# Exponentials of the attention stage: one step at a time, or two steps in one instruction behind two tanh

## The chip, the core and the metric

The kernel runs on one core of a Trainium2 chip. Its five engines work side by side, each through its own queue in order, and wait for each other by semaphores: TensorE (PE in the profile, PEld its weight loads), VectorE (DVE), ScalarE (ACT), GpSimd (POOL) and SyncE (SP), which here only issues transfers. The metric is the device time of one execution in microseconds (us), median of several runs.

## The reference, cut to what matters

Two layers of a small model, each an attention-like half times a gate. The first layer's attention is the part at hand: 4 sequences of 512 tokens, 8 heads, two sets of queries and keys of 8 dimensions per head.

```python
L1 = jnp.einsum('bhnd,bhmd->bhnm', _l2norm(q1), _l2norm(k1)) * cos_scale
L2 = jnp.einsum('bhnd,bhmd->bhnm', _l2norm(q2), _l2norm(k2)) * cos_scale
G = jnp.tanh(delta_gain.reshape(1, H, 1, 1) * (L1 - L2))
A1 = jax.nn.softmax(L1 + G, axis=-1)
A2 = jax.nn.softmax(L2 - G, axis=-1)
attn = A1 - lambda_full * A2
y = jnp.einsum('bhnm,bhmd->bhnd', attn, v)
```

The first layer's gate holds a mixture of 8 experts, one expert per token (`relu(x @ W1[e] + b1[e]) @ W2[e] + b2[e]`). Its blocks of 128 tokens run in between the steps of the attention. The second layer, a state-space model of four sublayers and another mixture of experts, comes behind it and isn't touched.

## The kernel before, in words

The attention stage runs over four pairs of heads (`pair_of_heads`: q = -1 unrolled and named `first`, q = 0 and 1 as a loop, q = 2 named `final`). A pair has 32 **steps**, a step being 128 keys by 512 queries of one head and one sequence. Four steps make a **unit** (one head and one sequence), so there are 32 units. From the second pair on, each unit u also carries one expert block: 24 units with a block, 8 without.

The work of step n:
- TensorE `difference` (L817): the differences L1 - L2 into `bank_d`, of which there are two; it waits until the tanh of step n - 2 has read the bank. `scores` (L822, L823): both logits into `bank_l`, two as well, free when VectorE has summed step n - 2.
- ScalarE `gate` (L923): tanh of `bank_d` into `gt`, a ring of 4. `exps` (L929 before): exponentials of `tt`, 1024 columns, into `ex`.
- VectorE `sums` (L978, L979): L1 + G and L2 - G (from the negated second logits) into `tt`, a ring of 4.

The work of unit u, done while later steps run:
- TensorE `weigh` (L863), in two halves of two steps: the values weighted by `ex`, into the single bank `bank_pv`.
- ScalarE `keep` (L934 before): a copy of `bank_pv` into `pvs`, behind the second half of weigh.
- TensorE `turn` (L871): four transposes of `pvs` back into `bank_pv`. VectorE `settle` (L986) reads them, and only then may the next unit's weigh begin.

The work of the expert block of unit u:
- TensorE `turn_block` (L838) into `bank_e`; ScalarE `keep_in` (L938 before) copies it to `block_inT`; TensorE `hidden` (L844); VectorE `relu` (L994); TensorE `block_out` (L850); ScalarE `keep_out` (L943 before) copies the result, and frees `bank_e` for the next block.

The order on each engine is written out by hand in the loops over steps. On TensorE, step st issues `difference` of st + 2, then `scores` of st + 1; at the first step of unit u also turn(u - 2) and turn_block(u), at the second hidden(u) and the first half of weigh(u - 1), at the third block_out(u) and the second half of weigh(u - 1). Here `pair_of_heads` runs u within a pair; a unit's turn is of the unit whose copy was made last.

Of the kernel before, what the change touches and what calls it, by code (L numbers as in the profile page):

```python
# [8 lines left out]
ACT = mybir.ActivationFunctionType  # L9
# [38 lines left out]
def build_stages(nc, A, out):  # L48
    keep = ExitStack()
    with keep:  # L50
        def sb(stack, name, shape, dtype=fp32):
            return stack.enter_context(nc.sbuf_tensor(name, shape, dtype))
# [22 lines left out]
        with keep0:  # L75
# [39 lines left out]
            with st1:  # L115
# [51 lines left out]
                with nc.Block() as block:  # L167
# [15 lines left out]
                    @block.sync  # L183
                    def _(sp):
                        for b in range(B):
                            sp.dma_start(X[:, 4 * b:4 * b + 4, :], A["x"][b].rearrange("(k p) d -> p k d", p=P)).then_inc(s_x[b], 16)
                        for dst, src in first_loads:
                            sp.dma_start(dst, src).then_inc(s_w, 16)
                        for dst, src in small_loads:
                            sp.dma_start(dst, src).then_inc(s_w2, 16)  # L190
                        for dst, src in loads:
                            sp.dma_start(dst, src).then_inc(s_w3, 16)
                        for h in range(NH):
                            sp.dma_start(sub_col[16 * h:16 * h + 16, :], A["subln"].rearrange("(d o) -> d o", o=1)).then_inc(s_b2l, 16)
                        sp.wait_ge(s_b2z, 1)
                        for t in range(NT):
                            sp.dma_start(b2blk[NE * t:NE * t + NE, t, :], A["b2"]).then_inc(s_b2l, 16)

                        for b in range(B):
                            sp.wait_ge(s_mid, 2 * b + 2)  # L200
                            sp.wait_ge(s_loq, b + 1)
                            sp.wait_ge(s_lok, b + 1)
                            for n, w in enumerate("qk"):
                                for i in range(3):
                                    sp.dma_start(columns(qk_dram[n, i], b), columns(parts[w, i], b)).then_inc(s_qkst, 16)
                        sp.wait_ge(s_qkst, 16 * 6 * B)
                        sp.wait_ge(s_z, 2)
                        for part in range(2):
                            load_part(sp, 0, 0, part, s_hl)
                        sp.wait_ge(s_hl, 16 * LOADS)  # L210
                        sp.wait_ge(s_b2l, 16 * (NT + NH))
# [420 lines left out]
            with st2:  # L632
                RING = 4
# [28 lines left out]
                tt = sb(st2, "tt", [P, RING, 2, 512])  # L662
                ex = sb(st2, "ex", [P, 2, 4, 2, 512])
# [9 lines left out]
                s_D, s_L, s_G, s_T, s_E = map(sem, ("diff_in_psum", "logits_in_psum2", "gate_ready", "sums_ready", "exp_ready"))  # L673
# [8 lines left out]
                LEAD, STEPS, UNITS, PER = 4, 32, 8, BLOCKS // 3  # L682
                step = lambda q, n: LEAD + STEPS + STEPS * q + n
# [5 lines left out]
                with nc.Block() as block:  # L689
# [220 lines left out]
                    @block.scalar  # L910
                    def _(act):
                        for s in (s_G, s_E, s_pvs, s_xk, s_ek):
                            act.sem_inc(s, LEAD)
                        for s in s_es:
                            act.sem_inc(s, 16)

                        def gate(q, st):
                            i = (st // 16) % 2
                            if st % 16 == 0:
                                act.wait_ge(s_dg, q * 2 + (st // 16 + 3))  # L920
                            act.wait_ge(s_D, step(q, st + 1))
                            act.wait_ge(s_T, step(q, st - RING + 1))
                            nc.scalar.activation(gt[:, st % RING, :], bank_d[st % 2][:, :], ACT.Tanh, scale=dgh[:, i:i + 1]).then_inc(s_G, 1)  # L923

                        def exps(q, st):
                            act.wait_ge(s_T, step(q, st + 1))
                            if st % 4 == 0:
                                act.wait_ge(s_pvd, unit(q, st // 4 - 1))
                            nc.scalar.activation(ex[:, (st // 4) % 2, st % 4, :, :], tt[:, st % RING, :, :], ACT.Exp).then_inc(s_E, 1)  # L929

                        def keep(q, u):
                            act.wait_ge(s_pvd, unit(q, u + 1))
                            act.wait_ge(s_pvt, unit(q, u))
                            nc.scalar.activation(pvs[:, :], bank_pv[:, :], ACT.Copy).then_inc(s_pvs, 1)  # L934

                        def keep_in(q, k):
                            act.wait_ge(s_xt, blk(q, k + 1))
                            nc.scalar.activation(xbT[:, :], bank_e[:, 0, :], ACT.Copy).then_inc(s_xk, 1)  # L938

                        def keep_out(q, k):  # L940
                            act.wait_ge(s_dn, blk(q, k + 1))
                            act.wait_ge(s_es[k % 2], loaded(q, k))
                            nc.scalar.activation(eo[k % 2][:, :], bank_e[:, 0, :], ACT.Copy).then_inc(s_ek, 1)  # L943

                        def pair_of_heads(q, first=False, final=False):
                            for st in range(STEPS):
                                u, mb = st // 4, st % 4
                                if not (final and st == STEPS - 1):
                                    gate(q, st + 1)
                                if not (first and st == 0):  # L950
                                    exps(q, st - 1)
                                if mb == 3 and not (first and u == 0):
                                    keep(q, u - 1)
                                if mb == 0 and not first:
                                    keep_in(q, u)
                                if mb == 3 and not first:
                                    keep_out(q, u)

                        gate(-1, 0)
                        pair_of_heads(-1, first=True)  # L960
                        with act.Fori(0, 2) as q:
                            pair_of_heads(q)
                        pair_of_heads(2, final=True)
                        exps(2, STEPS - 1)
                        keep(2, UNITS - 1)

                    @block.vector
# [971 lines left out]
        with st5:  # L1939
# [34 lines left out]
            first = lambda l, b: isinstance(l, int) and l == 0 and b == 0  # L1974
# [601 lines left out]
```

## Time and profile before

| | |
|---|---|
| device time, median of 3 runs | 1323.59 us (1323.31 to 1324.79) |
| span of the profiled execution (no device time is listed for it alone) | 1331.0 us |
| mean granted TensorE clock | 0.945 of 2.4 GHz |
| TensorE busy in the span | 1161.9 us (87%) |
| VectorE busy | 1103.2 us (83%) |
| ScalarE busy | 1051.4 us (79%) |
| GpSimd busy | 914.3 us (69%) |
| exps, 128 of 128x1024 | 138.4 us busy, 1081 ns mean |
| tanh, 128 of 128x512 | 91.3 us busy, 714 ns mean |

The span runs from the first to the last instruction that the profiler saw. The busy shares are means over stages with different limits: the attention stage lies between about 104 and 356 us of it and has limits of its own. A busy time of TensorE counts its pipelined matmuls with modelled ends, so that the distance between starts says more than the durations. The granted clock has two levels here, 1.00 (2.4 GHz) and 0.50 (1.2 GHz).

### The profile page before, as it was taken

Reading aid. Unit: us, or ns where it says so; the run is one execution under the profiler, and the core shown is the slowest. Engines: PE = TensorE matmul, PEld = TensorE weight load, DVE = VectorE, ACT = ScalarE, POOL = GpSimd, SP = SyncE. Lnnn points to the kernel's source line nnn. Section 1 sums busy time; section 2 is a strip of 40 time slices with the busy share of each in tenths; the row PEclk is TensorE's granted clock in tenths of the full one; section 3 lists DMA queues with packets and bytes.
Section 4 is the critical chain, followed back from the end, with each engine's and each line's share of the span. In section 5 each row is a group of like instructions: output and inputs, shape, how many; then the busy total and the mean of one; then the engine's idle time right before and its main releaser. Section 6 shows DMA issues by size and latency. Waiting matters only on the chain. (4 is left out here: it accounts for less than half of the span.)

```text
span 1331.0 us, 21677 instructions
## 1 busy us (share of the span) xinstructions
PE 1161.9 (87%) x6667; PEld 613.7 (46%) x6667; DVE 1103.2 (83%) x1535; ACT 1051.4 (79%) x1868; POOL 914.3 (69%) x749
## 2 busy tenths in 40 slices
PE   6566799999818999987999999999999999999885
PEld 4461144444414565663444444444444444444442
DVE  7966698999785323338999999999999999999997
ACT  4347799999743224359899999999999999999992
POOL 6734212111284442347999999999999999999995
PEclk9776799999966999998999999999999999999998
DMA  2122223433107305523345234423441444144420
GB/s 70 33 86 96 74 86 104 123 111 114 34 22 253 130 17 130 150 68 103 76 104 124 66 68 108 105 77 77 104 109 55 93 106 109 49 88 103 105 65 16
DMA packets 89061, 120.20 MB, mean 90 GB/s; under 512 B 17869, under 2 KB 49464, under 8 KB 88576
## 3 DMA queue, kind: packets, MB, share of 16 engines
q1 hardware_dynamic: 82688, 101.59, 30.0%
q0 software_dynamic: 6272, 17.38, 4.5%
q8 instruction: 48, 0.79, 0.3%
q14 instruction: 53, 0.43, 0.1%
HBM read 92.28 MB, written 27.45 MB: 90 GB/s over the span
## 5 line engine op out<-in xcount | busy, mean ns | idle before, releaser
L2094 POOL TENSOR_TENSOR hcm<-hs,Cc 128x1024 f32<-128x1024 f32 x255 | 600.8, 2379 | 27.5 <-DVE hs L2477 23.1
L2477 DVE TENSOR_TENSOR_SCAN hs<-decay,dbx 128x512 f32<-128x512 f32 x512 | 586.8, 1200 | 25.5 <-ACT decay L2370 9.5
L2211 PEld LDWEIGHTS dbx<-ident_sb,scaled 128*128 128x128 f32 x2048 | 227.7, 142 | 288.4 <-DVE hs L2477 164.4
L2211 PE MATMUL dbx<-ident_sb,scaled 128*128 128x128 f32 x2048 | 312.3, 283 | 41.4 <-DVE hs L2477 38.1
L2352 ACT ACTIVATE scaled<-duT,BT 128x256 f32<-128x256 f32 x579 | 266.9, 506 | 0.2 <-PE dbx L2211 0.2
L2370 ACT ACTIVATE decay<-dtr_even,a_all 128x512 f32<-128x512 f32 x256 | 178.6, 721 | 3.0 <-DVE hs L2477 1.7
L2370 ACT ACTIVATE decay<-dtr_odd,a_all 128x512 f32<-128x512 f32 x256 | 177.9, 721 | 2.3 <-DMA dtr_odd<-dt_turn 1.5
L929 ACT ACTIVATE ex<-tt 128x1024 f32<-128x1024 f32 x128 | 138.4, 1081 | 5.5 <-DVE tt L979 5.1
L2229 PE MATMUL y_bank<-hcm,fold_sb 128*32 128x512 f32 x1024 | 139.5, 617 | 2.1 <-POOL hcm L2094 2.1
L2142 PE MATMUL slots<-XT,w_tap 128*128 128x512 f32 (+1 forms) x224 | 115.4, 597 | 3.1 <-DVE scaled L2468 2.7
L978 DVE TENSOR_TENSOR tt<-bank_l,gt 128x512 f32<-128x512 f32 x128 | 87.4, 683 | 27.9 <-PE bank_l L823 19.2
L923 ACT ACTIVATE gt<-bank_d,dgh 128x512 f32<-128x512 f32 x128 | 91.3, 714 | 17.1 <-issue 7.6
L2079 POOL TENSOR_SCALAR scaled<-duT,BT 128x256 f32<-128x256 f32 x204 | 96.2, 485 | 0.0
L979 DVE SCALAR_TENSOR_TENSOR tt<-bank_l,gt 128x512 f32<-128x512 f32 x128 | 87.0, 680 | 0.0
L863 PE MATMUL bank_pv<-ex,v_head 128*32 128x512 f32 x512 | 72.1, 638 | 3.3 <-issue 2.8
L1839 DVE TENSOR_TENSOR hid<-sil,u_bank 128x512 f32<-128x512 f32 x32 | 22.0, 688 | 58.5 <-ACT sil L1696 30.8
L2468 DVE TENSOR_TENSOR scaled<-slots,BT 128x1024 f32<-128x1024 f32 (+1 forms) x60 | 67.8, 1131 | 0.0
L752 POOL CAST weight_rows<-w_row 128x1 uint32 (+1 forms) x24 | 4.5, 187 | 82.7 <-PE bank_e L850 82.7
L746 POOL COPY dgh<-delta_gain_sb 128x1 f32<-128x1 f32 (+1 forms) x8 | 1.4, 184 | 80.0 <-PE bank_pv L863 59.8
L1696 ACT ACTIVATE sil<-g_bank 128x512 f32<-128x512 f32 x32 | 19.1, 597 | 46.9 <-PE u_bank L1553 41.3
L1929 DVE TENSOR_TENSOR hid<-sil,u_bank 128x320 f32<-128x320 f32 x32 | 15.6, 488 | 48.7 <-ACT sil L1782 40.0
L1517 POOL DMA_INDIRECT shares_of_tokens<-eo,to_u x18 | 17.2, 956 | 51.8 <-ACT eo L1819 48.2
(379 smaller groups left out, 1938.0 us busy)
## 6 DMA issues: line engine op xcount, KB each, us to landing
Cc<-bc_turn SPq DMA_DIRECT2D x256, 64.0 KB
dtr_even<-dt_turn SPq DMA_DIRECT2D x32, 512.0 KB, 8.6
dtr_odd<-dt_turn SPq DMA_DIRECT2D x32, 512.0 KB, 8.4
dt_turn<-dt SPq DMA_DIRECT2D x16, 512.0 KB, 2.8
hid<-in_conv_row SPq DMA_DIRECT2D x4, 512.0 KB, 5.9
shares_of_tokens<-zeros SPq DMA_DIRECT2D x2, 1024.0 KB, 8.1
w_rg<-in_w_rg SPq DMA_DIRECT2D x8, 256.0 KB
w_ru<-in_w_ru SPq DMA_DIRECT2D x8, 256.0 KB
```

The source lines that it names most:

```text
L923: nc.scalar.activation(gt[:, st % RING, :], bank_d[st % 2][:, :], ACT.Tanh, scale=dgh[:, i:i + 1]).then_inc(s_G, 1)
L929: nc.scalar.activation(ex[:, (st // 4) % 2, st % 4, :, :], tt[:, st % RING, :, :], ACT.Exp).then_inc(s_E, 1)
L978: nc.vector.tensor_tensor(tt[:, st % RING, 0, :], bank_l[st % 2][:, 0, :], gt[:, st % RING, :], ALU.add)
L979: nc.vector.scalar_tensor_tensor(tt[:, st % RING, 1, :], bank_l[st % 2][:, 1, :], -1.0, gt[:, st % RING, :], ALU.mult, ALU.subtract).then_ ...
L2079: nc.gpsimd.tensor_scalar(scaled[buffer_of(l, n, k)][:, kk, :, j, :], duT[:, n % 2, kk, :].rearrange("p (g c) -> p g c", c=32), BT[:, n % ...
L2094: nc.gpsimd.tensor_tensor(hcm[:, r - 1:r + 1, :], hs[:, p % HR - 1:p % HR + 1, :], Cc[:, k:k + 1, :].broadcast_to([P, 2, 512]), ALU.mult). ...
L2142: last = mm(dst[h][:, d:512], w_tap[:, 3 - d, P * h:P * h + P], XT[:, n % 4, 0:512 - d], start=(d == 0), stop=(d == 3))
L2211: last = nc.tensor.transpose(dbx[bank_of[p]][:, P * kk:P * kk + P], scaled[buffer_of(l, b, k)][:, kk, g, :, :].rearrange("p j c -> p (j c) ...
L2229: last = mm(y_bank[h][32 * q:32 * q + 32, :], fold[:, :], hcm[:, ring_of(l, b, p + q), :], start=False, stop=(k == 3), tile_position=(0, 3 ...
L2352: nc.scalar.activation(scaled[buffer_of(l, n, k)][:, kk, :, j, :], duT[:, n % 2, kk, :].rearrange("p (g c) -> p g c", c=32), ACT.Copy, sca ...
L2370: nc.scalar.activation(dec[:, p % DR, :], dtr[b % 2][:, g, :], ACT.Exp, scale=a_all[:, l, 4 * g + k:4 * g + k + 1]).then_inc(s_dec, 1)
L2477: nc.vector.tensor_tensor_scan(hs[:, p % HR, :], dec[:, p % DR, :], dbx[bank_of[p]][:, :], 0.0, ALU.mult, ALU.add).then_inc(s_sc, 1)
```

## The change

ScalarE's code alone is changed. One instruction takes the exponentials of two steps, 2048 columns, and waits for the sums of both. Ahead of it stand the tanh of the next two steps. The copies of a unit move with it: `keep` and `keep_out` stand behind the exponentials of the unit's third and fourth step, `keep_in` stands behind two tanh and ahead of the exponentials.

```diff
-                        def exps(q, st):
-                            act.wait_ge(s_T, step(q, st + 1))
+                        def exps_of_two(q, st):
+                            act.wait_ge(s_T, step(q, st + 2))
                             if st % 4 == 0:
                                 act.wait_ge(s_pvd, unit(q, st // 4 - 1))
-                            nc.scalar.activation(ex[:, (st // 4) % 2, st % 4, :, :], tt[:, st % RING, :, :], ACT.Exp).then_inc(s_E, 1)
+                            i, j = st % RING, st % 4
+                            nc.scalar.activation(ex[:, (st // 4) % 2, j:j + 2, :, :], tt[:, i:i + 2, :, :], ACT.Exp).then_inc(s_E, 2)
...
                         def pair_of_heads(q, first=False, final=False):
-                            for st in range(STEPS):
+                            for st in range(0, STEPS, 2):
                                 u, mb = st // 4, st % 4
-                                if not (final and st == STEPS - 1):
-                                    gate(q, st + 1)
-                                if not (first and st == 0):
-                                    exps(q, st - 1)
-                                if mb == 3 and not (first and u == 0):
-                                    keep(q, u - 1)
+                                if not (final and st == STEPS - 2):
+                                    gate(q, st + 2)
+                                    gate(q, st + 3)
                                 if mb == 0 and not first:
                                     keep_in(q, u)
-                                if mb == 3 and not first:
+                                exps_of_two(q, st)
+                                if mb == 2 and not (first and u == 0):
+                                    keep(q, u - 1)
+                                if mb == 2 and not first:
                                     keep_out(q, u)
 
                         gate(-1, 0)
+                        gate(-1, 1)
                         pair_of_heads(-1, first=True)
                         with act.Fori(0, 2) as q:
                             pair_of_heads(q)
                         pair_of_heads(2, final=True)
-                        exps(2, STEPS - 1)
                         keep(2, UNITS - 1)
```

On ScalarE, in the loop over pairs, from the exponentials of a unit's third step to the next unit's first exponentials, before the change (`gt` is written by the tanh, `ex` by the exponentials, `pvs` by `keep`, `block_out` by `keep_out`, `block_inT` by `keep_in`):

```order
L929 ACTIVATE ex<-tt 128x1024
L932 REGISTER_ALU
L934 ACTIVATE pvs<-bank_pv 128x512
L942 ISA
L943 ACTIVATE block_out<-bank_e 128x128
L921 REGISTER_ALU
L923 ACTIVATE gt<-bank_d,dgh 128x512
L929 ACTIVATE ex<-tt 128x1024
L937 REGISTER_ALU
L938 ACTIVATE block_inT<-bank_e 128x128
```

The tanh of the next unit's second step stands behind both copies, and one step's exponentials lie between the copies of `keep` and `keep_in`. The same place after the change, from that same tanh of the next unit's second step on:

```order
L923 ACTIVATE gt<-bank_d,dgh 128x512
L930 ACTIVATE ex<-tt 128x2048
L933 REGISTER_ALU
L935 ACTIVATE pvs<-bank_pv 128x512
L943 ISA
L944 ACTIVATE block_out<-bank_e 128x128
L921 REGISTER_ALU
L923 ACTIVATE gt<-bank_d,dgh 128x512
L921 REGISTER_ALU
L923 ACTIVATE gt<-bank_d,dgh 128x512
L938 REGISTER_ALU
L939 ACTIVATE block_inT<-bank_e 128x128
```

That tanh and the exponentials of two steps now stand ahead of `keep`, and two tanh stand between `keep_out` and `keep_in`. On TensorE the order is the same before and after; from block_out of a unit to hidden of the next it reads:

```order
L850 MATMUL bank_e<-expert_weights,hid 128x128 x4
L863 MATMUL bank_pv<-ex,v_head 32x512 x4
L816 REGISTER_ALU
L817 MATMUL bank_d<-XT 128x512
L822 MATMUL bank_l<-XT 128x512
L823 MATMUL bank_l<-XT 128x512
L816 REGISTER_ALU
L817 MATMUL bank_d<-XT 128x512
L822 MATMUL bank_l<-XT 128x512
L823 MATMUL bank_l<-XT 128x512
L869 REGISTER_ALU
L871 MATMUL bank_pv<-ident_sb,pvs 128x128 x4
```

The first `bank_d` here is the one that the tanh of the next unit's second step reads; nothing moved, and it stands behind block_out and weigh and ahead of the turn.

## Rows read from the trace of the kernel before

**Rows 1.** Windows: us busy by engine (PE, PEld, DVE, ACT, POOL), PEclk, DMA.

```profile
168.00:350.80 182.80, 179.88 (x1194) 84.65 (x1186) 167.50 (x354) 174.67 (x269) 30.22 (x54) 1.00 0.34 102
```

**Rows 2.** Timeline of TensorE, one unit: start us, us, what, [idle before <-releaser].

```profile
200.82 1.06 PE L863 MATMUL bank_pv<-ex,v_head 128*32 128x512 f32 x8
201.82 0.39 PE L817 MATMUL bank_d<-GATE 112*128 112x512 bf16 x1
...
203.10 0.66 PE L871 MATMUL bank_pv<-ident_sb,pvs 128*128 128x128 f32 x4
203.60 0.27 PE L838 MATMUL bank_e<-ident_sb,block_in 128*128 128x128 f32 x1
203.71 0.38 PE L817 MATMUL bank_d<-GATE 112*128 112x512 bf16 x1
...
204.46 1.16 PE L844 MATMUL bank_e<-block_inT,expert_weights 128*128 128x128 f32 x8
205.55 1.06 PE L863 MATMUL bank_pv<-ex,v_head 128*32 128x512 f32 x8
206.55 0.39 PE L817 MATMUL bank_d<-GATE 112*128 112x512 bf16 x1
206.87 0.39 PE L822 MATMUL bank_l<-GATE 48*128 48x512 bf16 x1
...
207.19 1.16 PE L850 MATMUL bank_e<-expert_weights,hid 128*128 128x128 f32 x8
208.28 1.06 PE L863 MATMUL bank_pv<-ex,v_head 128*32 128x512 f32 x8
209.27 0.39 PE L817 MATMUL bank_d<-GATE 112*128 112x512 bf16 x1
```

**Rows 3.** Timeline of ScalarE in the same unit.

```profile
201.95 0.60 ACT L934 ACTIVATE pvs<-bank_pv 128x512 f32<-128x512 f32 x1 [0.34 <-PE bank_pv L863]
...
204.12 0.28 ACT L938 ACTIVATE block_inT<-bank_e 128x128 f32<-128x128 f32 x1
...
204.92 1.05 ACT L929 ACTIVATE ex<-tt 128x1024 f32<-128x1024 f32 x1
205.87 0.68 ACT L923 ACTIVATE gt<-bank_d,dgh 128x512 f32<-128x512 f32 x1
206.44 1.05 ACT L929 ACTIVATE ex<-tt 128x1024 f32<-128x1024 f32 x1
...
209.41 0.60 ACT L934 ACTIVATE pvs<-bank_pv 128x512 f32<-128x512 f32 x1 [0.25 <-PE bank_pv L863]
```

**Rows 4.** Groups by line and form: busy us, mean ns, idle before.

```profile
L2383 ACT ACTIVATE GATE<-GATE 128x2048 f32<-128x2048 f32 x1 | 1.9, 1919 | 0.0
```

**Rows 5.** Timeline of ScalarE, copies of units without expert blocks.

```profile
159.06 0.66 ACT L934 ACTIVATE pvs<-bank_pv 128x512 f32<-128x512 f32 x1
...
165.61 0.70 ACT L934 ACTIVATE pvs<-bank_pv 128x512 f32<-128x512 f32 x1
```

**Rows 6.** Timeline of TensorE around three waits for ScalarE.

```profile
158.35 0.39 PE L817 MATMUL bank_d<-GATE 112*128 112x512 bf16 x1 [0.53 <-ACT gt L923]
...
159.78 0.93 PE L871 MATMUL bank_pv<-ident_sb,pvs 128*128 128x128 f32 x4 [0.72 <-ACT pvs L934]
...
163.47 0.39 PE L817 MATMUL bank_d<-GATE 112*128 112x512 bf16 x1
...
172.94 0.66 PE L871 MATMUL bank_pv<-ident_sb,pvs 128*128 128x128 f32 x4 [0.72 <-ACT pvs L934]
```

**Rows 7.** Timeline of ScalarE, one wait early in the stage.

```profile
144.44 0.69 ACT L923 ACTIVATE gt<-bank_d,dgh 128x512 f32<-128x512 f32 x1 [7.61 <-issue]
```

**Rows 8.** Windows of 1 us: columns as in the first group.

```profile
159.00:160.00 1.00, 0.28 (x4) 0.23 (x3) 1.00 (x2) 1.00 (x3) 0.00 (x0) 1.00 0.05 20
162.00:163.00 1.00, 1.00 (x8) 0.00 (x0) 1.00 (x3) 1.00 (x2) 0.00 (x0) 0.50 0.00 0
173.00:174.00 1.00, 1.00 (x8) 0.66 (x8) 0.20 (x1) 1.00 (x2) 0.00 (x0) 1.00 0.00 0
```

## The prediction

> **What bounds the attention stage now.** I first read the busy shares of the stage from the second pair of heads on, 168 to 350.8 us [rows 1]: TensorE 179.9 of 182.8 us at the full granted clock, ScalarE 174.7, VectorE 167.5. All three are nearly full, so a change of order on one of them has to be followed through the others. Then I read one unit in order of time. A unit is four steps; I write D(n), L(n) for the difference and score matmuls of step n, G(n) for its tanh (`gate`), T(n) for VectorE's sums, and "exps" for the exponentials.
>
> TensorE runs, in a fixed order: at step 4u D(4u+2), L(4u+1), turn(u-2), the block's turn; at 4u+1 D(4u+3), L(4u+2), hidden(u), first half of weigh(u-1); at 4u+2 D(4u+4), L(4u+3), block_out(u), second half of weigh(u-1); at 4u+3 D(4u+5), L(4u+4). In the trace one unit lasts from the second half of weigh at 200.82 to the next at 208.28, 7.46 us, and the starts follow each other almost without a gap [rows 2]. TensorE is the bound, but by little.
>
> ScalarE's row for the same unit shows what the change touches [rows 3]. `keep` copies the values at 201.95, as soon as weigh ends, and is done at 202.55; G(4u+5) comes behind it. The turn that needs the copy starts at 203.10 [rows 2]: it has 0.55 us to spare. That number decides this case.
>
> **The change, part by part.** It removes 128 exps of 1024 columns and adds 64 of 2048. ScalarE starts its next instruction 0.95 us after an exps of 1024 columns that lasts 1.05, so 0.10 is overlapped [rows 3]. No exps of 2048 columns is in the trace; a Silu of 2048 columns, from SBUF to SBUF as the exps are, lasts 1.919 us [rows 4]. The bounds are twice the exps, 2.10, and the exps plus the step from a 512-column to a 1024-column instruction, 1.05 + (1.05 - 0.68) = 1.42. I take 1.92, the row of the same width, since another function on the same columns is nearer than another width. Less 0.10 it occupies 1.82, against 2 x 0.95 = 1.90: 0.08 saved per pair, 64 x 0.08 = 5.1 us if ScalarE alone decided.
>
> It moves two things, and these cost. In the old order G(4u+4), exps(4u+2), keep(u-1), keep_out(u) stood before G(4u+5). In the new order G(4u+4), G(4u+5), exps(4u+2 and 4u+3) stand before keep(u-1). G(4u+5) reads D(4u+5), and D(4u+5) stands on TensorE behind block_out(u) and the second half of weigh(u-1). ScalarE works in order, so it stands still in front of G(4u+5) until TensorE has finished that weigh, although the sums for the exps are long there; then it does G, then 1.82 us of exps, and only then the copy that turn(u-1) waits for. Before, D(4u+5) started at 201.82 and the copy at 201.95 [rows 2, 3]. After, the copy starts a tanh and an exps pair behind the end of D(4u+5). Meanwhile TensorE can only run L(4u+4), D(4u+6), L(4u+5), and then it waits at turn(u-1). Second, keep_in(u+1) now stands behind G(4u+6) and G(4u+7), and D(4u+7) stands on TensorE behind that same turn; so hidden(u+1), which needs keep_in, is late again.
>
> The new cycle, each from a start to the next start, runs from D(4u+5) to D(4u+9):
> D to G: 0.39 for D plus 0.07, the time from the end of weigh (208.28 + 1.06) to the copy at 209.41 [rows 2, 3]: 0.46.
> G to exps 0.57 (205.87 to 206.44) [rows 3]; exps pair to keep 1.82; keep to turn 0.72, from 159.06 to 159.78 in a unit where the turn did wait for it, less the 0.06 by which that copy lasted longer (0.66 against 0.60): 0.66 [rows 3, 5, 6].
> Turn to the block's turn to D(4u+7) 0.61; D to G(4u+7) 0.46; G to keep_in 0.57; keep_in to hidden 0.34 (204.12 to 204.46) [rows 2, 3].
> Hidden to weigh 1.09, weigh to D 1.00, D to L 0.32, L to block_out 0.32, block_out to weigh 1.09, weigh to D(4u+9) 0.99 [rows 2].
> Sum: 0.46 + 0.57 + 1.82 + 0.66 + 0.61 + 0.46 + 0.57 + 0.34 + 1.09 + 1.00 + 0.32 + 0.32 + 1.09 + 0.99 = 10.30 us. Against 7.46 that is 2.84 us a unit, and there are 24 units with expert blocks: 24 x 2.84 = **68.2 us**. The bounds of the exps move it by about 3 us up and, at 1.32 occupied, by 12 us down.
>
> The first eight units have no expert blocks. There the cycle is D to G 0.46, G 0.57, exps 1.82, keep to turn 0.66, turn 0.50, D and L 0.64, weigh 1.00, D and L 0.64, weigh 0.99: 7.28 us. In the old order these units took 6.55 us (copies at 159.06 and 165.61) [rows 5], ScalarE alone being full. So 0.73 for each of units 4 to 7, **2.9 us**. Units 1 to 3 lie ahead of a wait of 7.61 us at 144.44 that the profile explains by nothing it shows [rows 7]; it may absorb their loss. I take 0 for them and 8 as the other end, since VectorE's settle between the sums isn't in my cycle.
>
> **The clock.** The new unit leaves TensorE two gaps: D(4u+5), L, D, L last 4 x 0.32 = 1.28 us while the turn starts 0.46 + 0.57 + 1.82 + 0.66 = 3.51 after D(4u+5), a gap of 2.2 us; and before hidden another, 1.37 from D(4u+7) less 0.64 for D and L, 0.7 us. What gaps do here: after one of 0.72 us before the turn at 159.78, with another of 0.53 shortly ahead of it, the granted clock went from 1.00 to 0.50 (2.4 to 1.2 GHz), and the turn, D, L and weigh took 3.69 us to the D at 163.47 [rows 6, 8]. At full clock the same four take 0.50 + 0.32 + 0.32 + 1.00 = 2.14 [rows 2]. One such fall costs 1.55 us. After the same wait of 0.72 at 172.94 the clock stayed at 1.00 [rows 6, 8]. The new gaps are over twice as long, so falls are likely but not certain in each unit. Bounds: none, 0; one in each of 31 units, 48 us. I take two units in three of the 24: 16 x 1.55 = **25 us**, nearer to the upper end, as the gaps are nearer to those that brought the fall.
>
> **Sum.** 68.2 + 2.9 + 24.8 = 95.9 us. The stage ends later by that, and what follows begins only when the last engine has left the stage, so all of it is passed on. The profiled span of 1331.0 us is 7.4 above the median of the runs, 0.6%; I add the difference to the median: 1323.6 + 95.9 = **1420 us**.
>
> **Rivals.** *The clock stays up.* The same late copy, no falls: 1323.6 + 68.2 + 2.9 = 1395. For it: the unit of 172.94. Against it: the fall at 159.78 after shorter gaps. *The clock falls in every unit, the first ones too:* 68.2 + 8 + 48 = 124, so 1448, and more if a second fall comes in a unit.
>
> *The saving decides, faster.* ScalarE is 174.7 of 182.8 us busy, and if only its throughput counted, 5.1 us would be gained: 1318.5. It would come so if turn(u-1) could bear the later copy. It becomes later by the end of D, G and the exps pair, 201.82 + 0.46 + 0.57 + 1.82 = 204.67 against 201.95, which is 2.72 us, and the turn has 0.55 to spare; the exps pair would have to occupy under 0 us for that. I see no mechanism that gives it, save that ScalarE's wait in front of G(4u+5) isn't the one I read.
> On this the Trainium skill, "Perfetto Trace Analysis", section Optimizing Scalar/DVE Operations, says both: grouping into larger operations helps a saturated engine, and where an engine isn't saturated but causes bubbles on others, breaking up lets work end sooner. By its first half the time would be the 1318.5 of this rival; by its second the change goes the wrong way, and the trace bears out the second, with 0.55 us of slack at the turn.
>
> *No change:* TensorE would have to take in 2.84 us a unit from idle time that it has already; in the whole stretch it idles 182.8 - 179.9 = 2.9 us [rows 1].
>
> **Chances.** Late copy with falls of the clock in part of the units 0.55; with hardly any 0.25; in every unit or worse 0.14; faster 0.04; no change 0.02. The range reaches into both slower rivals: from 1384, the 1395 less most of the 12 us of the exps' lower bound, to 1452, a little over the worst case's 1448. A measurement of this kernel tells about 0.2% from no change: faster 0.04, same 0.02, slower 0.94.
>
> **What would show it.** In the changed trace: exps of 2048 columns of about 1.92 us; ScalarE idle about 2 us before every fourth tanh, released by bank_d; TensorE idle about 2.2 us before the turn, released by the copy, and 0.7 before hidden, released by block_inT; units of 10.3 us at full clock; the granted clock below 1 in parts of 168 to 440 us. Wrong would be: units under 9 us, a copy that starts before the exps pair's end, or falls of the clock that last through the stage.

## The result

The changed kernel takes 1458.85 us (median of 4 runs, 1454.41 to 1462.38) against 1324.19 us before (4 runs): 1.101 times as long, 95% interval 1.0986 to 1.1035. It is slower, as forecast, but by 134.7 us in place of 95.9, and outside the range, which ended at 1452.

The page of the changed kernel gives the busy time of each engine, and the groups by line and form of the attention stage give the two instructions of ScalarE (columns: busy us, mean ns of one, idle before and what ended it):

```profile
span 1458.6 us, 21645 instructions
...
PE 1220.8 (84%) x6667; PEld 639.8 (44%) x6667; DVE 1105.4 (76%) x1535; ACT 1052.3 (72%) x1804; POOL 915.2 (63%) x749
```

```profile
L930 ACT ACTIVATE ex<-tt 128x2048 f32<-128x2048 f32 x64 | 122.0, 1906 | 23.7 <-DVE tt L980 12.4 <-issue 11.3
...
L923 ACT ACTIVATE gt<-bank_d,dgh 128x512 f32<-128x512 f32 x128 | 87.7, 688 | 127.8 <-PE bank_d L817 117.2 <-DVE tt L980 10.7
```

An exps pair (the exponentials of two steps in one instruction) takes 1.906 us; the forecast took 1.92 from [rows 4]. What is new is the idle time ahead of the tanh, 127.8 us, of which 117.2 end when TensorE's `bank_d` arrives: ScalarE stands still there.

One unit of the loop, in order of time, answers to [rows 2] and [rows 3]. TensorE from the turn of one unit to the turn of the next (start us, us, what, in brackets the idle time before and what ended it):

```profile
280.05 0.66 PE L871 MATMUL bank_pv<-ident_sb,pvs 128*128 128x128 f32 x4 [2.10 <-ACT pvs L935]
...
282.06 2.07 PE L844 MATMUL bank_e<-block_inT,expert_weights 128*128 128x128 f32 x8 [0.70 <-ACT block_inT L939]
284.06 1.94 PE L863 MATMUL bank_pv<-ex,v_head 128*32 128x512 f32 x8
...
287.01 1.64 PE L850 MATMUL bank_e<-expert_weights,hid 128*128 128x128 f32 x8
288.58 1.06 PE L863 MATMUL bank_pv<-ex,v_head 128*32 128x512 f32 x8
289.58 0.39 PE L817 MATMUL bank_d<-XT 112*128 112x512 bf16 x1
...
293.03 0.65 PE L871 MATMUL bank_pv<-ident_sb,pvs 128*128 128x128 f32 x4 [2.10 <-ACT pvs L935]
```

ScalarE in the same unit:

```profile
290.01 0.69 ACT L923 ACTIVATE gt<-bank_d,dgh 128x512 f32<-128x512 f32 x1 [2.67 <-PE bank_d L817]
290.59 1.90 ACT L930 ACTIVATE ex<-tt 128x2048 f32<-128x2048 f32 x1
292.39 0.59 ACT L935 ACTIVATE pvs<-bank_pv 128x512 f32<-128x512 f32 x1
```

The forecast chain is there link by link. ScalarE waits 2.67 us for the D(4u+5) that TensorE starts at 289.58, behind block_out and weigh. G starts at 290.01 (0.43 after D), the pair 0.58 later, the copy 1.80 later, the turn 0.64 later. TensorE waits 2.10 us at the turn and 0.70 at hidden; the forecast said 2.2 and 0.7.

What the forecast sized wrongly is seen in the durations: hidden 2.07 us where [rows 2] has 1.16, weigh 1.94 where it has 1.06. The windows of the changed kernel (us busy of PE, PEld, DVE, ACT, POOL, then the granted clock, DMA) show why; the last is the whole loop, from the 8th to the 31st copy:

```profile
281.20:287.80 6.60, 5.90 (x24) 2.98 (x23) 4.25 (x10) 3.41 (x4) 0.00 (x0) 0.50 0.20 57
288.00:294.60 6.60, 4.24 (x28) 1.69 (x26) 2.55 (x5) 4.26 (x6) 1.73 (x4) 1.00 0.21 59
294.90:298.00 3.10, 3.04 (x16) 1.99 (x16) 1.75 (x6) 1.92 (x2) 0.00 (x0) 0.50 0.35 115
298.30:304.90 6.60, 4.50 (x30) 1.82 (x27) 4.65 (x9) 3.84 (x6) 1.20 (x2) 1.00 0.29 96
191.46:477.44 285.98, 226.21 (x1120) 106.18 (x1120) 160.46 (x333) 163.72 (x206) 28.31 (x50) 0.77 0.21 64
```

The clock falls to 1.2 GHz in the unit from 281, for over 6.6 us, and again in the next, for half as long. Over the loop its mean is 0.77, where [rows 1] has 1.00. The copies of `keep` on ScalarE give the length of the units; these are the first, the 8th, four in a row from the loop, and the 31st:

```profile
125.80 0.58 ACT L935 ACTIVATE pvs<-bank_pv 128x512 f32<-128x512 f32 x1
...
191.46 0.59 ACT L935 ACTIVATE pvs<-bank_pv 128x512 f32<-128x512 f32 x1
...
404.99 0.59 ACT L935 ACTIVATE pvs<-bank_pv 128x512 f32<-128x512 f32 x1
416.76 0.59 ACT L935 ACTIVATE pvs<-bank_pv 128x512 f32<-128x512 f32 x1
429.60 0.59 ACT L935 ACTIVATE pvs<-bank_pv 128x512 f32<-128x512 f32 x1
442.54 0.59 ACT L935 ACTIVATE pvs<-bank_pv 128x512 f32<-128x512 f32 x1
...
477.44 0.58 ACT L935 ACTIVATE pvs<-bank_pv 128x512 f32<-128x512 f32 x1
```

### The profile page after: what moved, and what is told of

Same layout as the page of the kernel before. It is cut to its first block and busy times, and to the rows that moved or that the text cites. A ratio compares the mean times of both kernels' runs of the same rounds, so it can differ in the third digit from the quotient of the medians.

```text
span 1458.6 us, 21645 instructions
## 1 busy us (share of the span) xinstructions
PE 1220.8 (84%) x6667; PEld 639.8 (44%) x6667; DVE 1105.4 (76%) x1535; ACT 1052.3 (72%) x1804; POOL 915.2 (63%) x749
## 5 line engine op out<-in xcount | busy, mean ns | idle before, releaser
L923 ACT ACTIVATE gt<-bank_d,dgh 128x512 f32<-128x512 f32 x128 | 87.7, 688 | 127.8 <-PE bank_d L817 117.2
L930 ACT ACTIVATE ex<-tt 128x2048 f32<-128x2048 f32 x64 | 122.0, 1906 | 23.7 <-DVE tt L980 12.4
L863 PE MATMUL bank_pv<-ex,v_head 128*32 128x512 f32 x512 | 93.4, 814 | 0.5 <-DVE ybig L987 0.5
L871 PE MATMUL bank_pv<-ident_sb,pvs 128*128 128x128 f32 x128 | 23.7, 313 | 64.7 <-ACT pvs L935 64.7
L987 DVE TENSOR_REDUCE ybig<-bank_pv 128x136 f32<-128x272 f32 (+1 forms) x32 | 14.1, 442 | 71.1 <-PE bank_pv L871 71.1
L844 PE MATMUL bank_e<-block_inT,expert_weights 128*128 128x128 f32 x192 | 49.8, 441 | 13.1 <-ACT block_inT L939 13.1
```

Source lines behind the costliest of these rows:

```text
L863: last = nc.tensor.matmul(bank_pv[32 * j:32 * j + 32, :], vh[i][:, 4 * b + mb, :], ex[:, u % 2, mb, s, :], start=(pair == 0), stop=(pair = ...
L930: nc.scalar.activation(ex[:, (st // 4) % 2, j:j + 2, :, :], tt[:, i:i + 2, :, :], ACT.Exp).then_inc(s_E, 2)
```

## The experiments

Ten other kernels were run, and the kernel before once more. Full clock in what follows is the granted clock 1.00. A unit is the distance of two copies of `keep` on ScalarE; "the loop" is the 23 units from the 8th to the 31st copy.

**The exponentials split again, order kept.**

```diff
-nc.scalar.activation(ex[:, (st // 4) % 2, j:j + 2, :, :], tt[:, i:i + 2, :, :], ACT.Exp).then_inc(s_E, 2)
+for k in range(2):
+    nc.scalar.activation(ex[:, (st // 4) % 2, j + k, :, :], tt[:, i + k, :, :], ACT.Exp).then_inc(s_E, 1)
```

> The changed order on ScalarE is kept, but the exponentials of two steps are again two instructions of 1024 columns, one behind the other. Theory A (the place of the copies behind the second tanh and both exponentials is the cause): the cycle is 10.3 us at full clock as before, 2 x 0.95 in place of 1.82, so the time stays near that of the change, 1450 to 1468 us. Theory B (the merged instruction is the cause, since it waits for the sums of both steps and holds ScalarE for 1.9 us): the time goes most of the way back, under 1350 us.

Measured: 1458.19 us, ratio to before 1.1019 (1.0981 to 1.1057), the same as the change. The merged instruction as such has no part in the loss of this order. Two things are the same in both runs, the order and the wait for the sums of both steps; of the second the changed trace shows little, 12.4 us of idle time ahead of all 64 pairs that VectorE's sums ended. The runs below change the order.

**TensorE's gaps filled with repeated matmuls.** The score matmuls of a step are repeated into the same bank, with the same result, so that TensorE is busy in the gaps. Each run has one of the three added lines; the loop that repeats the matmuls inside `scores` is left out here.

```diff
-scores(q, st + 1)
+scores(q, st + 1, {0: 7, 1: 3}.get(mb, 1))     # both gaps
+scores(q, st + 1, {0: 7, 1: 1}.get(mb, 1))     # the long gap alone
+scores(q, st + 1, {0: 1, 1: 3}.get(mb, 1))     # the short gap alone
```

> The change, with TensorE's two gaps in each unit filled by repeats of work that is done anyway: the score matmuls ahead of the turn run 7 times in place of once (6 x 0.32 = 1.9 us of the 2.1 us gap), those ahead of hidden 3 times (0.64 of 0.7 us). The result is the same numbers. Theory A (of the 4.99 us a unit, 2.8 are the late copy and 2.2 are the granted clock that falls in the gaps): the clock stays at 1.00 in the loop, units last 10.2 to 10.4 us, and the time is 1324 + 24 x 2.85 + 8 = 1400 us (1390 to 1412). Theory B (the extra 2.2 us are something else, such as waits between VectorE and ScalarE that the longer unit brings): units stay at 12 us or more and the time stays at 1450 us or above.

> The change with only the long gap ahead of the turn filled, by six repeats of the score matmuls (1.9 of 2.1 us); the short gap of 0.7 us ahead of hidden stays. If the long gap is what brings the falls, none are left: units of 10.2 us and 1400 to 1406 us, as with both gaps filled. If the short gap brings falls too, units above 11 us and 1415 us or more.

> Only the gap of 0.7 us ahead of hidden is filled, by two repeats of the score matmuls there; the gap of 2.1 us ahead of the turn stays. If the long gap makes the clock fall and the short one behind it keeps it low for twice as long (two of three units are 12.84 us, one is 11.77), every unit comes to 11.8 us or less and the time is 1435 us or less. If the long gap alone decides both, the time stays within 5 us of 1459.

Measured: 1401.01 us with both gaps filled (ratio 1.0582, 1.0564 to 1.06), 1401.07 with the long gap alone (1.0589, 1.0571 to 1.0606), 1412.78 with the short gap alone (1.0656, 1.0625 to 1.0687). More work on TensorE makes the kernel faster by 58 us. Copies of the run with both gaps filled, and windows of a stretch in it:

```profile
234.72 0.59 ACT L937 ACTIVATE pvs<-bank_pv 128x512 f32<-128x512 f32 x1
...
244.92 0.59 ACT L937 ACTIVATE pvs<-bank_pv 128x512 f32<-128x512 f32 x1
...
255.12 0.59 ACT L937 ACTIVATE pvs<-bank_pv 128x512 f32<-128x512 f32 x1
```

```profile
200.00:300.00 100.00, 89.99 (x639) 40.40 (x641) 66.67 (x139) 69.97 (x89) 13.34 (x24) 1.00 0.27 82
```

Units are 10.20 us and the clock is 1.00. The forecast cycle at full clock was 10.30. The repeats fill less than expected, since a repeated pair takes 0.22 us and not 0.32: 0.80 us of the long gap are left. The first, the 8th and the 31st copy of this run, and its turn in between:

```profile
126.30 0.59 ACT L937 ACTIVATE pvs<-bank_pv 128x512 f32<-128x512 f32 x1
...
183.74 0.59 ACT L937 ACTIVATE pvs<-bank_pv 128x512 f32<-128x512 f32 x1
...
255.76 0.66 PE L873 MATMUL bank_pv<-ident_sb,pvs 128*128 128x128 f32 x4 [0.80 <-ACT pvs L937]
...
417.34 0.58 ACT L937 ACTIVATE pvs<-bank_pv 128x512 f32<-128x512 f32 x1
```

The run with the long gap alone filled has the same units and the same clock, in the first line below. The same stretch of the run with the short gap alone filled has TensorE 79.33 us busy at a clock of 0.97, five stretches at half clock in its 23 units and most units at 10.20, in the second line:

```profile
200.00:300.00 100.00, 85.70 (x600) 38.98 (x592) 66.72 (x141) 70.85 (x89) 13.18 (x23) 1.00 0.28 83
200.00:300.00 100.00, 79.33 (x517) 36.65 (x515) 67.06 (x141) 67.47 (x85) 12.40 (x24) 0.97 0.25 76
```

So with this order the short gap alone brings no fall and the long one alone brings few; it takes both for one in every unit. The expectations of the first two runs came true. That of the third, 1435 us or less if the short gap prolongs the stretches, holds in its number, but it reckoned with a fall left in each unit: filling either gap is nearly enough.

**The difference matmul issued earlier.**

```diff
-if not (final and st >= STEPS - 2):
+if mb % 2 == 0 and not (final and st >= STEPS - 2):
     difference(q, st + 2)
 if not (final and st >= STEPS - 1):
     scores(q, st + 1)
+if mb % 2 == 0 and not (final and st >= STEPS - 2):
+    difference(q, st + 3)
```

> ScalarE as in the change; on TensorE the difference matmul that the second tanh waits for is issued two steps' matmuls earlier, behind the scores of the same step and ahead of the expert block and the weighting. Theory A (ScalarE stands still ahead of the second tanh because that matmul lies behind block_out and weigh, and the exponentials are held back with it): the pair of exponentials runs while TensorE does block_out and weigh, the copy follows weigh at once, units come to about 8.8 us at full clock, and the time is 1324 + 24 x 1.4 + 6 = 1363 us, up to 1400 if the clock still falls. Theory B (the copy is late because two steps' exponentials lie ahead of it, whatever the tanh waits for): little changes, 1440 us or more.

Measured: 1373.48 us, ratio 1.0386 (1.0364 to 1.0408). ScalarE's order is that of the change, and 85 of the 135 us are gone. Its timeline in this run, and TensorE's turn behind the copy:

```profile
256.83 1.25 ACT L925 ACTIVATE gt<-bank_d,dgh 128x512 f32<-128x512 f32 x2
258.93 1.91 ACT L932 ACTIVATE ex<-tt 128x2048 f32<-128x2048 f32 x1 [0.85 <-DVE tt L982]
260.75 0.58 ACT L937 ACTIVATE pvs<-bank_pv 128x512 f32<-128x512 f32 x1
```

```profile
261.38 0.66 PE L871 MATMUL bank_pv<-ident_sb,pvs 128*128 128x128 f32 x4 [1.09 <-ACT pvs L937]
```

The two tanh run back to back, and the exponentials wait 0.85 us for the sums in place of 2.67 for the matmul. Units are 8.75 to 8.9 us where the clock holds, 9.16 in the mean. Against the 10.20 us of the change at full clock this gives back about 1.4 us a unit, half of what the change cost there; the rest of the 85 us is the clock, which falls seven times in the loop in place of 23. The expected unit of 8.8 us came out, but not the reason, that the copy follows weigh at once: TensorE's second half of weigh starts at 257.93 here, and the pair only at 258.93. What stays is that the copy comes behind the pair, and TensorE waits 1.09 us for it at the turn, in the last line.

**The copies moved back ahead.** On ScalarE alone: `keep` and `keep_out` between the two tanh; `keep_in` ahead of both; and both moves together.

This is the run with both, its conditions left out. The run with `keep` early leaves `keep_in` where it was, the run with `keep_in` early leaves `keep` and `keep_out`.

```diff
+keep_in(q, u)
 gate(q, st + 2)
+keep(q, u - 1)
+keep_out(q, u)
 gate(q, st + 3)
-keep_in(q, u)
 exps_of_two(q, st)
-keep(q, u - 1)
-keep_out(q, u)
```

> The change with keep and keep_out moved between the two tanh: they stand behind the first tanh of the pair and ahead of the second tanh and the exponentials. keep_in stays behind two tanh. Theory A (two waits make the late unit, the turn's for keep and hidden's for keep_in): the first is gone, the second stays, since keep_in still stands behind the tanh that reads the matmul behind the turn; units come to about 9.4 us at full clock, 1324 + 24 x 1.95 + 2 = 1373 us, up to 1420 with falls of the clock. Theory B (keep alone makes the unit late): units near 7.5 us and a time under 1335 us.

> The change with keep_in alone moved ahead of both tanh; keep and keep_out stay behind the pair of exponentials. The wait ahead of hidden goes and the wait of 2.1 us ahead of the turn stays: about 9.5 us a unit at full clock, 1324 + 24 x 2.05 + 8 = 1381 us if the clock stays up, up to 1420 if the long gap alone brings falls. If one late copy were enough for all of the loss, it would stay at 1450 us.

> As the run with keep early, and keep_in moved ahead of both tanh as well, where the block's turn releases it. Theory A: both waits are gone, what remains is that the exponentials of two steps wait for the later step's sums; units of about 8.25 us at full clock, 1324 + 24 x 0.8 = 1343 us, up to 1375 with falls. Theory B (the merged exponentials cost nothing once the copies are early): units at 7.46 us or less and a time of 1318 to 1326 us.

Measured: 1393.18 us with `keep` early (ratio 1.052, 1.0489 to 1.0551), 1418.89 with `keep_in` early (1.0721, 1.0687 to 1.0756), 1344.50 with both (1.0144, 1.0116 to 1.0172). With one copy late, one gap of about 2.1 us remains, once ahead of hidden and once ahead of the turn; TensorE's waits in the first and in the second:

```profile
253.18 1.16 PE L844 MATMUL bank_e<-block_inT,expert_weights 128*128 128x128 f32 x8 [2.06 <-ACT block_inT L939]
...
262.65 2.08 PE L844 MATMUL bank_e<-block_inT,expert_weights 128*128 128x128 f32 x8 [2.06 <-ACT block_inT L939]
```

```profile
252.73 0.66 PE L871 MATMUL bank_pv<-ident_sb,pvs 128*128 128x128 f32 x4 [2.10 <-ACT pvs L935]
```

The units with `keep` early are 9.46 and 11.02 us in turn: the unit of 262.65 runs hidden at half clock. With `keep_in` early they are 9.50 at full clock and 11.0 to 12.5 with a fall. Windows of the two runs, `keep` early first:

```profile
200.00:320.00 120.00, 96.22 (x577) 46.46 (x577) 80.46 (x170) 80.43 (x105) 15.05 (x30) 0.91 0.27 83
200.00:320.00 120.00, 96.93 (x551) 47.62 (x555) 76.79 (x162) 80.59 (x101) 15.20 (x28) 0.87 0.25 78
```

So either late copy alone costs 2.0 us a unit at full clock, and both together 2.7. With both copies early the clock stays up (1.00 from 200 to 320 us) and a unit is 8.31 us, expected 8.25. TensorE still waits 0.90 us in each, for `keep_in`, which stands behind the pair. The reason given in the expectation, that the pair waits for the later step's sums, isn't in the trace: from 200 to 320 us ScalarE has no idle time ahead of its 30 pairs, and stands still only ahead of `keep`. The number came out, the reason didn't:

```profile
250.09 1.16 PE L844 MATMUL bank_e<-block_inT,expert_weights 128*128 128x128 f32 x8 [0.90 <-ACT block_inT L939]
...
258.40 1.16 PE L844 MATMUL bank_e<-block_inT,expert_weights 128*128 128x128 f32 x8 [0.90 <-ACT block_inT L939]
```

**The difference matmul and the copies both earlier.** TensorE as in the run with the difference matmul earlier; ScalarE `keep_in`, two tanh, `keep`, `keep_out`, the pair (conditions left out).

```diff
+keep_in(q, u)
 gate(q, st + 2)
 gate(q, st + 3)
-keep_in(q, u)
-exps_of_two(q, st)
 keep(q, u - 1)
 keep_out(q, u)
+exps_of_two(q, st)
```

> TensorE issues the difference matmuls two steps at a time (the second ahead of the expert block and the weighting), and ScalarE has keep_in first, then two tanh, keep, keep_out, and the pair of exponentials last. Theory A: units of about 8.0 us at full clock, 1324 + 24 x 0.55 = 1337 us (1328 to 1352), still slower than before, since TensorE was full in the loop and the pair of exponentials can only add waits there. Theory B (the saving on ScalarE shows once nothing waits for the copies): 1312 to 1320 us.

Measured: 1332.66 us, ratio 1.0067 (1.0045 to 1.0088). Two copies, and TensorE's wait between them:

```profile
256.59 0.60 ACT L937 ACTIVATE pvs<-bank_pv 128x512 f32<-128x512 f32 x1 [1.02 <-PE bank_pv L863]
...
259.38 1.16 PE L844 MATMUL bank_e<-block_inT,expert_weights 128*128 128x128 f32 x8 [0.69 <-ACT block_inT L941]
...
264.45 0.60 ACT L937 ACTIVATE pvs<-bank_pv 128x512 f32<-128x512 f32 x1 [1.02 <-PE bank_pv L863]
```

The unit is 7.86 us against 7.46 [rows 2]. It is the best order with pairs in the loop that was tried, and it is still slower than before: TensorE was full there and has nothing to gain, and it waits 0.69 us at hidden in each unit.

**Pairs in the first eight units alone,** the loop as before (`exps_of_two` is added as in the change).

```diff
-pair_of_heads(-1, first=True)
+gate(-1, 1)
+for st in range(0, STEPS, 2):
+    u, mb = st // 4, st % 4
+    gate(-1, st + 2)
+    if mb == 2 and u > 0:
+        keep(-1, u - 1)
+    if st < STEPS - 2:
+        gate(-1, st + 3)
+        exps_of_two(-1, st)
+    else:
+        exps(-1, st)
```

> The kernel before in all but the first pair of heads, the eight units without expert blocks, where ScalarE was full: there the exponentials of two steps are one instruction, with keep ahead of the second tanh. Theory A (the saving of a merged instruction shows only where ScalarE is the bound): units 4 to 7 go from 6.55 to about 6.4 us, 1 us in all, 1323 us; and if the wait of 7.6 us early in the stage, which the changed kernel's trace doesn't have, hangs on where ScalarE's code stands, up to 8 us more, 1315 us. Theory B (merging makes waits for the later step's sums here too): 1325 to 1335 us.

Measured: 1325.23 us, ratio 1.0005 (0.999 to 1.0021), no change that can be told. Its copies:

```profile
126.45 0.59 ACT L941 ACTIVATE pvs<-bank_pv 128x512 f32<-128x512 f32 x1
...
132.81 0.63 ACT L941 ACTIVATE pvs<-bank_pv 128x512 f32<-128x512 f32 x1
...
139.17 0.67 ACT L941 ACTIVATE pvs<-bank_pv 128x512 f32<-128x512 f32 x1
```

These are units of 6.36 us against 6.55 [rows 5]: 0.19 us saved where ScalarE is the bound, 0.10 a pair where the forecast had 0.08. It is there, over some five units, and too small for the measurement. The further 8 us hoped for didn't come.

**The kernel before, profiled once more.**

> The kernel before, unchanged, for a second profile. Theory A (the wait of 7.6 us at ScalarE early in the stage, and the longer wait around it, belong to that one profiled execution: its span of 1331.0 us is 7.4 above the median of the runs): no such wait here, the first eight copies lie about 51 us apart from first to last in place of 59.7, and the span is about 1322 us. Theory B (it is in every execution): the wait is there again and the span is about 1331 us.

Measured: span 1323.2 us, one time of 1324.95. The wait of 7.61 us [rows 7] isn't in this execution. Its first and eighth copy are 53.09 us apart; the third line is the 31st:

```profile
118.76 0.58 ACT L934 ACTIVATE pvs<-bank_pv 128x512 f32<-128x512 f32 x1
...
171.85 0.60 ACT L934 ACTIVATE pvs<-bank_pv 128x512 f32<-128x512 f32 x1 [0.51 <-PE bank_pv L863]
...
342.98 0.60 ACT L934 ACTIVATE pvs<-bank_pv 128x512 f32<-128x512 f32 x1
```

In the profile that the forecast was made from the first and the eighth copy are 59.7 apart. That execution carried a wait that none of the other profiled ones has. It doesn't count in full. The copies on its two sides are 17.18 us apart, 10.6 more than their neighbours, but from the first to the eighth copy that execution is only 6.7 us longer: the second profile has a wait of its own later among these units, on TensorE, for a transfer:

```profile
158.39 0.61 PE L817 MATMUL bank_d<-XT 112*128 112x512 bf16 x1 [2.94 <-DMA XT<-qk_parts]
```

## Why the prediction was wrong in size

Against the second profile of before, the 135.4 us between the spans (1458.6 and 1323.2) fall as follows, by the first tanh and the copies of the two traces. The stage starts 4.2 us later (107.58 against 103.38; nothing ahead of it was changed, in the other runs it lies between 103.37 and 104.81, and what this one execution waited for stays open). From there to the first copy it is 18.2 against 15.4 us, 2.8 more. From the first to the eighth copy 65.66 against 53.09, 12.6 more. In the loop 285.98 against 171.13, **114.9 more**. Behind it 0.9 more.

**The bound and the slack: right.** TensorE was full and the turn had 0.55 us to spare; the traces show the new waits of 2.10 and 0.70 us at the two places named.

**The cycle of 10.30 us: right.** With the gaps filled the clock holds and the unit is 10.20. Of the loop's 114.9 us this is 23 x (10.16 - 7.44) = 62.6; the forecast had 68.2 for 24 units. The runs with the copies early show that it is the order, and the run with the earlier difference matmul shows that the stop ahead of the second tanh is about half of it. One side sum is off and changes nothing: the upper bound of the exps, 2.00 occupied in place of 1.82, moves 24 units by 4.3 us, not by 3.

**The clock: the step that failed.** The forecast took 25 us for it, one fall of 1.55 us in two units of three. Measured, the mean unit is 12.43 us against 10.16 with the gaps filled: 2.27 us a unit, 52 us in the loop. The trace has 23 stretches at half clock in those 23 units, 133 of 286 us in all. Units of 11.77 us are 1.57 over the full-clock unit, which is the price of one fall taken from [rows 6]; the others, two of three, are 12.84 to 12.98, 2.6 to 2.8 over it. So the price of a short stretch was right, the count was too low, and that a stretch can last twice as long wasn't in the sum nor in its upper end, which had one fall of that price in every unit. One of the forecast's own signs of being wrong, "falls of the clock that last through the stage", is there in the loop. With 52 us in the loop and about 8 in the first units, where filling the gaps takes 65.66 us between copies down to 57.44, the clock costs some 60 us in place of 25. The row of 172.94 in [rows 6], where it stayed up, was weighed too heavily: there a wait of 0.72 us stood in the place of these 2.10.

**The first eight units: too low.** Forecast 2.9 us, measured 12.6 + 2.8. Of the 12.6, 8.2 go with the clock, as said, and 4.4 stay with the gaps filled (57.44 against 53.09). At full clock the unit there is 7.81 us (the distance most found with the gaps filled) against 6.54, 1.27 a unit where the forecast took 0.73; VectorE's settle, named there as left out, lies in that cycle. The units 1 to 3 lose like the others: the wait of 7.61 us that might have absorbed them belongs to one execution. Seven such units would make 8.9 us and not 4.4; a likely reason is the wait of 2.94 us for a transfer in the kernel before, which the trace with the gaps filled, later by then, doesn't have.

**The rivals.** That the saving decides is out, as the early copies show too: with both copies early and the matmul too the pairs still cost 0.4 us a unit in the loop. None of the kernels tried is faster than the one before. Of the two sentences of the Trainium skill weighed there ("Perfetto Trace Analysis", Optimizing Scalar/DVE Operations), on larger operations and on breaking them up, neither is what decided here: breaking up the pair without moving it left the time at 1458.19 us. "The clock falls in every unit" was held at 0.14 and is what happened, at 1448 by the forecast's price and 1459 measured.

Which gaps bring a fall, and which make a stretch last twice as long, is only partly settled. In the loops with gaps of 0.69, 0.80 and 0.90 us the clock stays at 1.00; with one of about 1.1 it falls seven times in 23 units. It takes both gaps for the pattern of the changed kernel, but one gap of 2.06 ahead of hidden brings a fall in every second unit, and one of 2.10 ahead of the turn five with the short gap filled and 17 with `keep_in` early. The work around the gap differs in these runs, and no run here varies that alone.

## What to carry to other kernels

On an engine that works in order, ask of an instruction moved ahead what it waits for and what then stands behind it: here a tanh or two and a pair of exponentials moved ahead of two copies of 0.6 and 0.3 us cost 2.7 us a unit at TensorE, for a saving of 0.1 us per pair. Where TensorE is full and at full clock, a new gap can be paid twice, as the gap itself and as half clock behind it; price the second from a stretch at half clock, for every repetition and for stretches longer than the one in the trace. And take a second profile before an unexplained wait goes into a sum.

## What the runs showed that was not expected

- Repeating a pair of score matmuls in TensorE's gaps, work that is thrown away, made the changed kernel 58 us faster (1458.85 to 1401.01), through the granted clock (0.78 to 1.00 from 200 to 300 us).
- Filling one of the two gaps is nearly as good as filling both: 1401.07 us with the long one, 1412.78 with the short one.
- Repeats of the pair start 0.22 us apart, where a pair and the next difference matmul take 0.32.
- Two executions of the same kernel differ by a wait of 7.61 us in one place on ScalarE; the profile alone doesn't say what it waited for.
